# Piecewise-linear softmax weights: row maximum subtracted on TensorE, slopes carried in diagonal matrices, another engine order

## Chip, cores and metric

The program runs on one core of one Trainium2 chip. The metric is device time in microseconds (us) for one execution of the whole program, a small tower of four attention layers and four feed-forward layers over 2784 tokens of width 192. The change touches one stage of the second attention layer (the "pla" stage, `14_pla_...` in the names of the trace).

## The reference, cut to what matters

Scores of 12 heads are turned into attention weights by a softmax whose exponential is a table of straight lines (twelve pieces on -10 to 0, the last of them never chosen), after the shifted scores are put on a grid of 2^-26:

```python
scores = jnp.einsum('bhqd,bhkd->bhqk', q, k) * scale
def pla_softmax(scores):
    m = jnp.max(scores, axis=-1, keepdims=True)
    shifted = to_fixed_point(scores - m, 32, 26)      # round(x * 2**26), clipped, / 2**26
    xc = jnp.clip(shifted, -10.0, 0.0)
    idx = jnp.clip(jnp.searchsorted(PLA_A, xc, side='right') - 1, 0, PLA_A.shape[0] - 2)
    exps = PLA_M[idx] * xc + PLA_C[idx]
    sm = exps / (jnp.sum(exps, axis=-1, keepdims=True) + 1e-09)
    return quant(to_fixed_point(sm, 16, 15))
```

The pieces are 10/12 wide, so three of them span 2.5, and lines that lie 2.5 apart differ by the factor exp(-2.5). The kernel uses that: it moves each shifted score up by a whole number of steps of 2.5 into the pieces 8 to 10, evaluates those three lines, and multiplies by exp(-2.5 x steps).

## The kernel before, in words

`pla_stage` (L2483), called from `l1_attn` (L2925), works in 16 units of two batches each. One unit is a tile of 128 partitions by 1479 columns: 17 chunks of 87 keys, one row maximum for each chunk and partition. In PSUM such a tile lies in four banks, three with 435 columns (`wide`) and one with 174 (`rest`), so most PSUM reads are two instructions. Five engines run their own program, ordered by semaphores; each engine takes its instructions strictly in the order written out in the loops at the end of its function.

For a unit j:

- SyncE spreads the queries of a unit into block form with 12 DMAs (`heads.spread`), two units ahead of the scores at most.
- TensorE: `score(j)` puts the scores in the PSUM tile `ps` (bf16, short). It may overwrite `ps` once VectorE has taken the unit before (`taken`).
- VectorE, `take_off_top` (L2605): the row maximum (two reductions, L2608, L2610), the maximum times the scale (L2612), scores times scale minus maximum into `raw` (two scalar_tensor_tensor from PSUM, L2617, L2621), and the clamp at -10 that also writes integers into the same memory, `less` (L2624).
- ScalarE: `count`, the number of steps (L2581), and `fall`, exp(-2.5 x count) (L2585).
- VectorE, `shift` (L2637): `v` = `less` + 2.5 x `count`, two buffers.
- ScalarE: three lines over `v`, each a full pass with its own slope and offset: `mid` (L2589), `high` (L2591), `low` (L2593), two buffers each.
- VectorE, `cut` (L2628, L2630): `mid` and `high` are set to zero below their edges.
- TensorE, `add_up` (L2539): low, mid and high are added in the PSUM tile `line`, by matmuls with the identity, in fp32. One such pass over a tile is four matmuls in the source and eight in the trace, since fp32 takes two each (six of L2543, two of L2544).
- VectorE, `scale_line` (L2647): `line` times `fall` into `f`; `sum_up` (L2655 to L2662): the row sums and their reciprocals.
- ScalarE, `share_out` (L2573): `f` times the reciprocal into the 16-bit weights, 17 instructions, two units later.

The order on VectorE in an iteration is: take_off_top(j), cut(j-1), shift(j), sum_up(j-2), scale_line(j-1). On TensorE: low, mid, high of unit j-1, then score(j+1). On ScalarE: count, fall, mid, high, low of unit j, then share_out(j-2).

## Time and profile before

| | us |
|---|---|
| median of three runs | 2383.24 (2379.29 to 2392.43) |
| the profiled execution | 2381.72 |
| its span in the trace | 2379.3 |

The first row is the number that a changed kernel is held against. The profiled execution is a single one of the same program, and its span is what the trace covers of it, 2.4 us less than its device time. The pla stage lies between about 816 and 1055 us of that span.

### The profile page before, as it was taken

Reading aid. Unit: us, or ns where it says so; the run is one execution under the profiler, and the core shown is the slowest. Engines: PE = TensorE matmul, PEld = TensorE weight load, DVE = VectorE, ACT = ScalarE, POOL = GpSimd, SP = SyncE. Lnnn points to the kernel's source line nnn. Section 1 sums busy time; section 2 is a strip of 40 time slices with the busy share of each in tenths; the row PEclk is TensorE's granted clock in tenths of the full one; section 3 lists DMA queues with packets and bytes.
Section 4 is the critical chain, followed back from the end, with each engine's and each line's share of the span. In section 5 each row is a group of like instructions: output and inputs, shape, how many; then the busy total and the mean of one; then the engine's idle time right before and its main releaser. Section 6 shows DMA issues by size and latency. Waiting matters only on the chain. (4 is left out here: it accounts for less than half of the span.)

```text
span 2379.3 us, 35751 instructions
## 1 busy us (share of the span) xinstructions
PE 1676.9 (70%) x12022; PEld 1359.0 (57%) x12038; DVE 1323.9 (56%) x2732; ACT 1044.3 (44%) x2115; POOL 344.1 (14%) x417
## 2 busy tenths in 40 slices
PE   3588879947751377656589686664793699469995
PEld 2266658636641244336579563443683598369995
DVE  6599962350147989978712467997326211542223
ACT  4477742302224678876112147884322254312221
POOL 0000000006630000001043100000000342034431
PEclk9799969877875588987689896775897699679998
DMA  3200010304440000000467300000003453446775
GB/s 85 69 19 18 21 26 4 83 24 136 138 157 1 4 6 6 5 1 2 124 215 215 125 4 8 7 4 1 13 1 109 141 181 116 138 133 223 225 215 190
DMA packets 137245, 189.81 MB, mean 80 GB/s; under 512 B 51661, under 2 KB 111214, under 8 KB 137070
## 3 DMA queue, kind: packets, MB, share of 16 engines
q1 hardware_dynamic: 116289, 146.91, 20.2%
q0 software_dynamic: 15360, 36.72, 5.3%
q10 hardware_dynamic: 5420, 3.91, 0.6%
q8 instruction: 102, 1.67, 0.3%
q14 instruction: 74, 0.60, 0.1%
HBM read 150.21 MB, written 33.68 MB: 77 GB/s over the span
## 5 line engine op out<-in xcount | busy, mean ns | idle before, releaser
L989 DVE TENSOR_TENSOR 36_l3f_mlp_hidden<-36_l3f_mlp_gate,36_l3f_mlp_first 128x512 f32<-128x512 f32 x51 | 35.1, 688 | 185.3 <-ACT 36_l3f_mlp_gate L967 104.6
L882 PE MATMUL 36_l3f_mlp_first<-36_l3f_mlp_xT,36_l3f_mlp_w 128*128 128x128 f32 x816 | 101.5, 278 | 1.9 <-issue 1.9
L1005 DVE TENSOR_SCALAR 9_l0f_mlp_y<-9_l0f_mlp_second,l0f_routing_weight 128x192 f32<-128x192 f32 x51 | 20.4, 416 | 142.7 <-PE 9_l0f_mlp_second L896 63.1
L882 PEld LDWEIGHTS 36_l3f_mlp_first<-36_l3f_mlp_xT,36_l3f_mlp_w 128*128 128x128 f32 x816 | 97.0, 195 | 1.6 <-issue 1.6
L1245 PE MATMUL 2_performer_p_u<-perf_proj,2_performer_yT 128*87 128x512 f32 (+1 forms) x204 | 88.8, 577 | 10.6 <-DVE 2_performer_arg L1406 9.4
L967 ACT ACTIVATE 36_l3f_mlp_gate<-36_l3f_mlp_first 128x512 f32<-128x512 f32 x51 | 30.5, 598 | 137.5 <-PE 36_l3f_mlp_first L887 128.3
L1003 DVE TENSOR_TENSOR 32_l3a_mlp_y<-32_l3a_mlp_second,l3a_experts_b_rows 128x192 f32<-128x192 f32 x29 | 10.4, 358 | 136.8 <-issue 102.2
L896 PE MATMUL 36_l3f_mlp_second<-l3f_experts_w,36_l3f_mlp_hidden 128*128 x408 | 80.9, 342 | 0.0
L989 DVE TENSOR_TENSOR 22_l1f_mlp_hidden<-22_l1f_mlp_gate,22_l1f_mlp_first 128x512 f32<-128x512 f32 x29 | 20.0, 688 | 106.4 <-ACT 22_l1f_mlp_gate L967 85.5
L963 ACT ACTIVATE 32_l3a_mlp_hidden<-32_l3a_mlp_first,l3a_experts_b_cols 128x128 f32<-128x128 f32 x174 | 48.3, 378 | 65.9 <-PE 32_l3a_mlp_first L887 51.7
L2573 ACT ACTIVATE l1a_p<-14_pla_f,l1a_recip 128x87 int16<-128x87 f32 x272 | 71.7, 356 | 4.9 <-DVE l1a_recip L2662 4.9
L2543 PE MATMUL 14_pla_line<-14_pla_low,ident 128*128 128x435 f32 x96 | 50.5, 673 | 29.9 <-ACT 14_pla_low L2593 27.6
L896 PE MATMUL 9_l0f_mlp_second<-l0f_experts_w,9_l0f_mlp_hidden 128*128 x204 | 55.4, 401 | 22.2 <-issue 12.2
L856 POOL DMA_INDIRECT l3f_results<-36_l3f_mlp_y,l3f_routing_put x51 | 50.3, 987 | 136.0 <-DVE 36_l3f_mlp_y L1005 136.0
L896 PEld LDWEIGHTS 36_l3f_mlp_second<-l3f_experts_w,36_l3f_mlp_hidden 128*128 128x128 f32 x408 | 65.9, 192 | 6.5 <-issue 0.5
L896 PE MATMUL 32_l3a_mlp_second<-l3a_experts_w,32_l3a_mlp_hidden 128*128 x348 | 66.0, 341 | 2.4 <-ACT 32_l3a_mlp_hidden L963 2.4
L2543 PE MATMUL 14_pla_line<-14_pla_mid,ident 128*128 128x435 f32 x96 | 41.1, 564 | 36.2 <-DVE 14_pla_mid L2628 36.2
L963 ACT ACTIVATE 9_l0f_mlp_hidden<-9_l0f_mlp_first,l0f_experts_b_cols 128x128 f32<-128x128 f32 x102 | 32.1, 364 | 76.5 <-PE 9_l0f_mlp_first L887 43.0
L1245 PEld LDWEIGHTS 2_performer_p_u<-perf_proj,2_performer_yT 128*87 128x87 f32 x204 | 31.8, 169 | 56.4 <-issue 53.8
L930 ACT ACT_TABLE_LOAD x4 | 5.1, 1283 | 133.1 <-PEq L605 92.9
L887 PE MATMUL 36_l3f_mlp_first<-36_l3f_mlp_xT,36_l3f_mlp_w 64*128 64x128 f32 x816 | 60.5, 287 | 0.8 <-issue 0.8
L896 PEld LDWEIGHTS 32_l3a_mlp_second<-l3a_experts_w,32_l3a_mlp_hidden 128*128 128x128 f32 x348 | 57.4, 194 | 6.1 <-issue 2.9
(910 smaller groups left out, 4950.3 us busy)
## 6 DMA issues: line engine op xcount, KB each, us to landing
36_l3f_mlp_w<-in_L_ffn_w_dram SPq DMA_DIRECT2D x51, 768.0 KB
22_l1f_mlp_w<-in_L_ffn_w_dram SPq DMA_DIRECT2D x29, 768.0 KB
32_l3a_mlp_w<-in_L_attn_W_dram SPq DMA_DIRECT2D x29, 576.0 KB
9_l0f_mlp_w<-in_L_ffn_down_w_dram SPq DMA_DIRECT2D x51, 192.0 KB
l3a_experts_w<-in_L_attn_W_dram SPq DMA_DIRECT2D x8, 576.0 KB
l1a_blocks<-l1a_qkb SPq DMA_DIRECT2D x192, 5.4 KB, 1.8
l1f_experts_w<-in_L_ffn_w_dram SPq DMA_DIRECT2D x8, 384.0 KB, 6.3
l2a_blocks<-l2a_qkb SPq DMA_DIRECT2D x192, 5.4 KB, 1.8
```

Source lines behind the costliest of these rows:

```text
L856: nc.gpsimd.indirect_dma_start(route.results, to(i), y[i % NY][:], None).then_inc(put[i % NY], 16)
L882: nc.tensor.matmul(to(t + a * PAIRS), of[:, t + a * PAIRS, :], at[:, 0, :], start=(t == 0), stop=True, skip_group_check=True)
L887: ins = nc.tensor.matmul(to(t + a * PAIRS), of[rows, 2 * PAIRS + t, :], at[rows, 1, :], start=False, stop=True, skip_group_check=True)
L896: ins = nc.tensor.matmul(second[j % 2][:, 0:D], hidden[j % 2][:, t, :], ex.w2[:, ds(expert[j], 1), t, :].rearrange("p a w -> p (a w)"), st ...
L963: ins = nc.scalar.activation(out[:, t], src[:, t // PAIRS, t % PAIRS, :], func, bias=ex.b1_cols[:, ds(e, 1), t])
L967: nc.scalar.activation(out[:], src[:, 0, 0:HT, :], func).then_inc(done, 1)
L989: v.tensor_tensor(hidden[j % 2][:], gate[j % 2][:], first[j % 2][1][:, 0, 0:HT, :], ALU.mult).then_inc(hidden_done, 1)
L1003: ins = v.tensor_tensor(y[i % NY][:], of, ex.b2_rows[:, ds(e, 1), :].rearrange("p a w -> p (a w)"), ALU.add)
L1005: ins = v.tensor_scalar(y[i % NY][:], of, route.weight[:, i:i + 1], None, ALU.mult)
L1245: ins = t.matmul(p_u[:, k, 0:(EIGHT - h) * M], yT[b % 2][:, k, :], proj[:, h:EIGHT, :].rearrange("p h m -> p (h m)"), start=True, stop=True)
L2543: nc.tensor.matmul(to_w[:, n], kit.ident[:], of_w[:, n], start=start, stop=stop)
L2573: ins = a(P[:, j, n, :], f[j % 2][:, n * NT:(n + 1) * NT], ACT.Copy, scale=recip[:, j, n:n + 1])
```

## The change

The same weights are computed with other steps, and the work is handed to the engines in another order.

- The row maximum is taken of the raw scores (`find_top`), without the multiplication by the scale. TensorE subtracts it inside PSUM: `take_off_top` adds minus one times the maximum, repeated along the 87 keys, to `ps` with a diagonal matrix `minus` (four fp32 matmuls in the source). ScalarE then copies the difference out times the scale (`take`, two activations).
- The clamp (`clamp`) also adds a constant HOME, so that zero of the moved value lies where lines 8 and 9 cross.
- The slopes go into three diagonal matrices `by_low`, `by_mid`, `by_high`, made once at the start by four small tensor_scalar instructions (with `minus`). So low needs no instruction before TensorE, mid is one cut of `v`, and high is `v` plus a constant on ScalarE (`move_high`) and a cut. The common constant BASE is added in `scale_line`, which becomes a scalar_tensor_tensor.
- `v`, `mid` and `high` have one buffer instead of two.
- The loops are rewritten: scores and the subtraction run two units ahead of the lines, low one unit ahead, sum_up follows scale_line of the same unit, and share_out comes one unit later instead of two.

```diff
-    edge = [float(np.float32(a) * np.float32(UNIT)) for a in A]
+    across_89, across_910 = ((c[n + 1] - c[n]) / (m[n + 1] - m[n]) for n in (8, 9))
+    HOME = float(np.float32(across_89 * UNIT))
+    GAP = float((across_910 - across_89) * UNIT)
+    LEAST_V = 64.0 * math.ceil((HOME - 10.0 * UNIT) / 64.0)
+    BASE = float(c[8] - m[8] * across_89)
+    edge = [float(np.float32(float(np.float32(a) * np.float32(UNIT)) + HOME)) for a in A]
...
-        v_row = [kit.sb(ctx, f"v{u}", [128, UW]) for u in range(2)]
+        v_row, mid, high = (kit.sb(ctx, n, [128, UW]) for n in ("v", "mid", "high"))
-        low, mid, high = ([kit.sb(ctx, f"{n}{u}", [128, UW]) for u in range(2)] for n in ("low", "mid", "high"))
...
-        bias = kit.sb(ctx, "bias", [128, 4])
+        bias = kit.sb(ctx, "bias", [128, 2])
+        minus, by_low, by_mid, by_high = (kit.sb(ctx, n, [128, 128]) for n in ("minus", "by_low", "by_mid", "by_high"))
...
-            for k, value in enumerate((c[8], c[9] - c[8], c[10] - c[9], A[8] / STEP + 0.5)):
+            for k, value in enumerate((A[8] / STEP + 0.5 + HOME / (STEP * UNIT), GAP)):
...
-                    pe.wait_ge(taken, j)
+                    pe.wait_ge(raw_ready, j)
...
-            def add_up(part, start, stop):
+            def take_off_top(j):
+                pe.wait_ge(top_found, 2 * j + 2)
+                wide, rest = in_banks(ps)
+                for n in range(3):
+                    nc.tensor.matmul(wide[:, n], minus[:], across(top[:, n * PER_BANK:(n + 1) * PER_BANK], 2, NT), start=False,
+                                     stop=True, skip_group_check=True)
+                nc.tensor.matmul(rest, minus[:], across(top[:, 3 * PER_BANK:CHUNKS], 2, NT), start=False, stop=True,
+                                 skip_group_check=True).then_inc(less_done, 1)
+            def add_up(by, part, start, stop):
                 to_w, to_r = in_banks(line)
                 of_w, of_r = in_row(part)
                 for n in range(3):
-                    nc.tensor.matmul(to_w[:, n], kit.ident[:], of_w[:, n], start=start, stop=stop)
-                return nc.tensor.matmul(to_r, kit.ident[:], of_r, start=start, stop=stop)
-
-            pe.wait_ge(cleared, 1)
+                    nc.tensor.matmul(to_w[:, n], by[:], of_w[:, n], start=start, stop=stop)
+                return nc.tensor.matmul(to_r, by[:], of_r, start=start, stop=stop)
+
+            def low_line(j):
+                pe.wait_ge(v_ready, j + 1)
+                if j >= 1:
+                    pe.wait_ge(f_ready, j)
+                add_up(by_low, v_row, True, False).then_inc(low_done, 1)
+
+            def mid_line(j):
+                pe.wait_ge(mid_cut, j + 1)
+                add_up(by_mid, mid, False, False).then_inc(mid_done, 1)
+
+            def high_line(j):
+                pe.wait_ge(high_cut, j + 1)
+                add_up(by_high, high, False, True).then_inc(line_done, 1)
+
+            pe.wait_ge(cleared, 5)
             score(0)
-            for j in range(UNITS + 1):
-                i = j - 1
-                if i >= 0:
-                    pe.wait_ge(low_ready, i + 1)
-                    if i >= 1:
-                        pe.wait_ge(f_ready, i)
-                    add_up(low[i % 2], True, False)
-                    pe.wait_ge(mid_cut, i + 1)
-                    add_up(mid[i % 2], False, False)
-                    pe.wait_ge(high_cut, i + 1)
-                    add_up(high[i % 2], False, True).then_inc(line_done, 1)
-                if j + 1 < UNITS:
-                    score(j + 1)
+            for j in range(-2, U):
+                if has(j + 2) and j + 2 >= 1:
+                    score(j + 2)
+                if has(j):
+                    mid_line(j)
+                    high_line(j)
+                if has(j + 2):
+                    take_off_top(j + 2)
+                if has(j + 1):
+                    low_line(j + 1)
 
...
-            act.wait_ge(made, 4)
+            act.wait_ge(made, 2)
...
+            def take(j):
+                act.wait_ge(less_done, j + 1)
+                if j >= 1:
+                    act.wait_ge(v_ready, j)
+                for to, of in zip(in_row(raw), in_banks(ps)):
+                    ins = a(to, of, ACT.Copy, scale=scale)
+                ins.then_inc(raw_ready, 1)
+
+            def count_steps(j):
+                act.wait_ge(less_ready, j + 1)
+                a(count[:], less, ACT.Relu, bias=bias[:, 0:1], scale=-1.0 / (STEP * UNIT)).then_inc(count_ready, 1)
+                act.wait_ge(count_ready, j + 1)
+                if j >= 2:
+                    act.wait_ge(f_ready, j - 1)
+                a(fall[j % 2][:], count[:], ACT.Exp, scale=-STEP).then_inc(fall_ready, 1)
 
...
-            for j in range(UNITS):
-                u = j % 2
-                act.wait_ge(less_ready, j + 1)
+            def move_high(j):
+                act.wait_ge(v_ready, j + 1)
                 if j >= 1:
-                    act.wait_ge(fall_ready, j)
-                a(count[:], less, ACT.Relu, bias=bias[:, 3:4], scale=-1.0 / (STEP * UNIT)).then_inc(count_ready, 1)
-                act.wait_ge(count_ready, j + 1)
-                if j >= 2:
-                    act.wait_ge(f_ready, j - 1)
-                a(fall[u][:], count[:], ACT.Exp, scale=-STEP).then_inc(fall_ready, 1)
-                act.wait_ge(v_ready, j + 1)
-                if j >= 2:
-                    act.wait_ge(line_done, j - 1)
-                a(mid[u][:], v_row[u][:], ACT.Identity, bias=bias[:, 1:2],
-                  scale=float((m[9] - m[8]) / UNIT)).then_inc(mid_ready, 1)
-                a(high[u][:], v_row[u][:], ACT.Identity, bias=bias[:, 2:3],
-                  scale=float((m[10] - m[9]) / UNIT)).then_inc(high_ready, 1)
-                a(low[u][:], v_row[u][:], ACT.Identity, bias=bias[:, 0:1], scale=float(m[8] / UNIT)).then_inc(low_ready, 1)
-                if j >= 2:
-                    share_out(j - 2)
-            share_out(UNITS - 2)
-            share_out(UNITS - 1)
-            act.wait_ge(stored, UNITS)
+                    act.wait_ge(line_done, j)
+                a(high[:], v_row[:], ACT.Identity, bias=bias[:, 1:2]).then_inc(high_ready, 1)
+
+            for j in range(-2, U + 1):
+                if has(j + 1):
+                    count_steps(j + 1)
+                if has(j - 1):
+                    share_out(j - 1)
+                if has(j + 1):
+                    move_high(j + 1)
+                if has(j + 2):
+                    take(j + 2)
+            act.wait_ge(stored, U)
...
-            def take_off_top(j):
+            def find_top(j):
                 wide, rest = in_banks(ps)
                 dve.wait_ge(scores_done, j + 1)
+                if j >= 1:
+                    dve.wait_ge(less_done, j)
                 v.tensor_reduce(top[:, 0:15].rearrange("r (c n) -> r c n", c=3),
                                 wide.rearrange("r c (n k) -> r c n k", k=NT), AX.X, ALU.max).then_inc(top_found, 1)
                 v.tensor_reduce(top[:, 15:CHUNKS], by_chunk(rest), AX.X, ALU.max).then_inc(top_found, 1)
-                dve.wait_ge(top_found, 2 * j + 2)
-                v.tensor_scalar(top[:], top[:], scale, None, ALU.mult).then_inc(top_ready, 1)
-                dve.wait_ge(top_ready, j + 1)
+
+            def clamp(j):
+                dve.wait_ge(raw_ready, j + 1)
+                v.tensor_scalar(less, raw[:], HOME, LEAST_V, ALU.add, ALU.max).then_inc(less_ready, 1)
+
+            def cut(j):
+                dve.wait_ge(v_ready, j + 1)
                 if j >= 1:
-                    dve.wait_ge(v_ready, j)
-                to_w, to_r = in_row(raw)
-                v.scalar_tensor_tensor(to_w.rearrange("r c (n k) -> r c n k", k=NT),
-                                       wide.rearrange("r c (n k) -> r c n k", k=NT), scale,
-                                       across(top[:, 0:15].rearrange("r (c n) -> r c n", c=3), 3, NT),
-                                       ALU.mult, ALU.subtract)
-                v.scalar_tensor_tensor(by_chunk(to_r), by_chunk(rest), scale, across(top[:, 15:CHUNKS], 2, NT),
-                                       ALU.mult, ALU.subtract).then_inc(taken, 1)
-                dve.wait_ge(taken, j + 1)
-                v.tensor_scalar(less, raw[:], -10.0 * UNIT, None, ALU.max).then_inc(less_ready, 1)
-
-            def cut(j):
-                dve.wait_ge(mid_ready, j + 1)
-                v.scalar_tensor_tensor(mid[j % 2][:], v_row[j % 2][:], edge[9], mid[j % 2][:], ALU.is_ge, ALU.mult).then_inc(mid_cut, 1)
+                    dve.wait_ge(mid_done, j)
+                v.scalar_tensor_tensor(mid[:], v_row[:], edge[9], v_row[:], ALU.is_ge, ALU.mult).then_inc(mid_cut, 1)
                 dve.wait_ge(high_ready, j + 1)
-                v.scalar_tensor_tensor(high[j % 2][:], v_row[j % 2][:], edge[10], high[j % 2][:], ALU.is_ge, ALU.mult).then_inc(high_cut, 1)
+                v.scalar_tensor_tensor(high[:], v_row[:], edge[10], high[:], ALU.is_ge, ALU.mult).then_inc(high_cut, 1)
 
             def shift(j):
                 dve.wait_ge(count_ready, j + 1)
-                if j >= 2:
-                    dve.wait_ge(low_ready, j - 1)
-                    dve.wait_ge(high_cut, j - 1)
-                v.scalar_tensor_tensor(v_row[j % 2][:], count[:], STEP * UNIT, less, ALU.mult,
-                                       ALU.add).then_inc(v_ready, 1)
+                if j >= 1:
+                    dve.wait_ge(low_done, j)
+                    dve.wait_ge(high_cut, j)
+                v.scalar_tensor_tensor(v_row[:], count[:], STEP * UNIT, less, ALU.mult, ALU.add).then_inc(v_ready, 1)
 
...
-                    ins = v.tensor_tensor(to, of, by, ALU.mult)
+                    ins = v.scalar_tensor_tensor(to, of, BASE, by, ALU.add, ALU.mult)
...
             v.memset(ps[:], 0.0).then_inc(cleared, 1)
-            dve.wait_ge(cleared, 1)
-            for j in range(UNITS + 2):
-                if j < UNITS:
-                    take_off_top(j)
-                if 1 <= j <= UNITS:
-                    cut(j - 1)
-                if j < UNITS:
-                    shift(j)
-                if j >= 2:
-                    sum_up(j - 2)
-                if 1 <= j <= UNITS:
-                    scale_line(j - 1)
+            for to, by in ((minus, -1.0), (by_low, m[8] / UNIT), (by_mid, (m[9] - m[8]) / UNIT), (by_high, (m[10] - m[9]) / UNIT)):
+                v.tensor_scalar(to[:], kit.ident[:], float(by), None, ALU.mult).then_inc(cleared, 1)
+            dve.wait_ge(cleared, 5)
+            for j in range(-2, U):
+                if has(j + 1):
+                    clamp(j + 1)
+                if has(j):
+                    cut(j)
+                if has(j + 2):
+                    find_top(j + 2)
+                if has(j + 1):
+                    shift(j + 1)
+                if has(j):
+                    scale_line(j)
+                    sum_up(j)
```

## Rows read from the trace of the kernel before

**Rows 1.** The page's first part: engine, busy us, share of the span, instructions.

```profile
PE 1676.9 (70%) x12022; PEld 1359.0 (57%) x12038; DVE 1323.9 (56%) x2732; ACT 1044.3 (44%) x2115; POOL 344.1 (14%) x417
```

**Rows 2.** Busy time by stretch: stretch, its length, engines' busy us, granted clock, DMA.

```profile
core 0: us, PE busy (x) PEld busy (x) DVE busy (x) ACT busy (x) POOL busy (x), PEclk, DMA share, GB/s
942.00:956.00 14.00, 10.77 (x46) 5.90 (x45) 13.79 (x17) 12.11 (x25) 0.00 (x0) 0.88 0.03 5
...
984.00:998.00 14.00, 9.19 (x46) 5.30 (x45) 13.79 (x16) 12.10 (x25) 0.00 (x0) 1.00 0.03 5
```

**Rows 3.** Timeline, one unit on VectorE: start us, us, instruction.

```profile
931.08 0.93 DVE L2624 TENSOR_SCALAR 14_pla_raw<-14_pla_raw 128x1479 int32<-128x1479 f32 x1
931.92 1.69 DVE L2628 SCALAR_TENSOR_TENSOR 14_pla_mid<-14_pla_v,14_pla_mid 128x1479 f32<-128x1479 f32 x1
...
935.14 1.69 DVE L2637 SCALAR_TENSOR_TENSOR 14_pla_v<-14_pla_count,14_pla_raw 128x1479 f32<-128x1479 int32 x1
...
936.75 1.68 DVE L2655 TENSOR_REDUCE 14_pla_parts<-14_pla_f 128x51 f32<-128x1479 f32 x1
...
939.10 1.70 DVE L2647 TENSOR_TENSOR 14_pla_f<-14_pla_line,14_pla_fall 128x1305 f32<-128x1305 f32 x2
...
940.71 1.51 DVE L2608 TENSOR_REDUCE 14_pla_top<-14_pla_ps 128x15 f32<-128x1305 f32 x1
...
942.50 0.24 DVE L2612 TENSOR_SCALAR 14_pla_top<-14_pla_top,l1a_sc 128x17 f32<-128x17 f32 x1
...
942.78 1.58 DVE L2617 SCALAR_TENSOR_TENSOR 14_pla_raw<-14_pla_ps,l1a_sc,14_pla_top 128x1305 f32<-128x1305 f32 x1
...
944.69 0.93 DVE L2624 TENSOR_SCALAR 14_pla_raw<-14_pla_raw 128x1479 int32<-128x1479 f32 x1
```

**Rows 4.** Timeline, the same unit's line passes on TensorE, idle time before in brackets.

```profile
933.67 2.47 PE L2543 MATMUL 14_pla_line<-14_pla_mid,ident 128*128 128x435 f32 x6 [1.63 <-DVE 14_pla_mid L2628]
...
936.27 2.36 PE L2543 MATMUL 14_pla_line<-14_pla_high,ident 128*128 128x435 f32 x6
...
938.46 0.46 PE L2544 MATMUL 14_pla_line<-14_pla_high,ident 128*128 128x174 f32 x2
...
941.29 3.76 PE L2543 MATMUL 14_pla_line<-14_pla_low,ident 128*128 128x435 f32 x6 [1.58 <-ACT 14_pla_low L2593]
```

**Rows 5.** Timeline, ScalarE in the same unit.

```profile
939.72 1.51 ACT L2593 ACTIVATE 14_pla_low<-14_pla_v,14_pla_bias 128x1479 f32<-128x1479 f32 x1
...
941.14 4.49 ACT L2573 ACTIVATE l1a_p<-14_pla_f,l1a_recip 128x87 int16<-128x87 f32 x17
```

**Rows 6.** Timeline, ScalarE in a later attention stage, score banks taken from PSUM.

```profile
1500.57 1.34 ACT L3306 ACTIVATE 25_log_int_raw<-25_log_int_ps,l2a_con 128x1305 int32<-128x1305 f32 x1
1501.80 0.40 ACT L3307 ACTIVATE 25_log_int_raw<-25_log_int_ps,l2a_con 128x174 int32<-128x174 f32 x1
```

**Rows 7.** Groups by form, TensorE in that later stage: busy us, mean ns.

```profile
L3255 PE MATMUL 25_log_int_mid<-25_log_int_top,25_log_int_minus 128*128 128x440 bf16 x48 | 23.0, 534 | 0.0
...
L3253 PE MATMUL 25_log_int_mid<-25_log_int_score,identb 128*128 128x512 bf16 x18 | 10.0, 579 | 45.7 <-ACT 25_log_int_square L3334 44.4 <-DVE 25_log_int_top L3390 1.3
```

**Rows 8.** Waits of the DMA queue in the stage: us in total, times, longest.

```profile
SPq L2452 <- PE 14_pla_ps L2424: 69.2, 12, 7.4
```

**Rows 9.** Timeline, the stage's first two units.

```profile
819.99 1.52 DVE L2608 TENSOR_REDUCE 14_pla_top<-14_pla_ps 128x15 f32<-128x1305 f32 x1 [1.74 <-PE 14_pla_ps L2424]
...
832.10 0.93 DVE L2624 TENSOR_SCALAR 14_pla_raw<-14_pla_raw 128x1479 int32<-128x1479 f32 x1
...
832.65 4.34 PE L2543 MATMUL 14_pla_line<-14_pla_low,ident 128*128 128x435 f32 x6 [6.32 <-ACT 14_pla_low L2593]
```

**Rows 10.** Timeline, the stage's last units.

```profile
1022.99 2.46 PE L2543 MATMUL 14_pla_line<-14_pla_low,ident 128*128 128x435 f32 x6 [1.58 <-ACT 14_pla_low L2593]
...
1026.39 0.93 DVE L2624 TENSOR_SCALAR 14_pla_raw<-14_pla_raw 128x1479 int32<-128x1479 f32 x1
...
1050.34 4.49 ACT L2573 ACTIVATE l1a_p<-14_pla_f,l1a_recip 128x87 int16<-128x87 f32 x17 [4.13 <-DVE l1a_recip L2662]
```

More of the change, by code:

```diff
@@ L2491, in pla_stage @@
     STEP = 2.5
-    edge = [float(np.float32(a) * np.float32(UNIT)) for a in A]
+    across_89, across_910 = ((c[n + 1] - c[n]) / (m[n + 1] - m[n]) for n in (8, 9))
[4 more added lines that the diff above has]
+    edge = [float(np.float32(float(np.float32(a) * np.float32(UNIT)) + HOME)) for a in A]
+    U = UNITS
     with kit.stage("pla") as ctx:
@@ L2504, in pla_stage @@
         parts = kit.sb(ctx, "parts", [128, CHUNKS, 3])
-        bias = kit.sb(ctx, "bias", [128, 4])
+        bias = kit.sb(ctx, "bias", [128, 2])
+        minus, by_low, by_mid, by_high = (kit.sb(ctx, n, [128, 128]) for n in ("minus", "by_low", "by_mid", "by_high"))
         ps = kit.ps(ctx, "ps", [128, 4, 512])
         line = kit.ps(ctx, "line", [128, 4, 512])
-        names = ("made", "scores_done", "top_found", "top_ready", "taken", "less_ready", "count_ready", "fall_ready",
-                 "v_ready", "mid_ready", "high_ready", "low_ready", "mid_cut", "high_cut", "line_done", "f_ready",
+        names = ("made", "scores_done", "top_found", "less_done", "raw_ready", "less_ready", "count_ready", "fall_ready",
+                 "v_ready", "high_ready", "mid_cut", "high_cut", "low_done", "mid_done", "line_done", "f_ready",
                  "parts_ready", "summed", "total_ready", "recip_ready", "stored", "cleared")
-        (made, scores_done, top_found, top_ready, taken, less_ready, count_ready, fall_ready, v_ready, mid_ready,
-         high_ready, low_ready, mid_cut, high_cut, line_done, f_ready, parts_ready, summed, total_ready,
+        (made, scores_done, top_found, less_done, raw_ready, less_ready, count_ready, fall_ready, v_ready, high_ready,
+         mid_cut, high_cut, low_done, mid_done, line_done, f_ready, parts_ready, summed, total_ready,
          recip_ready, stored, cleared) = (kit.sem(ctx, n) for n in names)
@@ L2516, in pla_stage @@
         K_v = QK[:, 1].rearrange("p k (b t) -> p k b t", t=NT)
+        has = lambda j: 0 <= j < U
         @block.gpsimd
         def _(pool):
-            for k, value in enumerate((c[8], c[9] - c[8], c[10] - c[9], A[8] / STEP + 0.5)):
+            for k, value in enumerate((A[8] / STEP + 0.5 + HOME / (STEP * UNIT), GAP)):
                 nc.gpsimd.memset(bias[:, k:k + 1], float(value)).then_inc(made, 1)
@@ L2524, in _ @@
         def _(sp):
-            for j in range(1, UNITS):
+            for j in range(1, U):
                 if j >= 2:
```

## The prediction

> **What bounds the kernel now.** The page's first part [rows 1] says only that no engine is busy for more than 70% of the whole span, so the stage has to be read by itself. The busy time by stretch comes next [rows 2]: in the middle of the pla stage VectorE is busy for 13.79 of 14 us, TensorE for 9.2 to 10.8 and ScalarE for 12.1. VectorE bounds this stage. Its timeline over one unit [rows 3] shows where that goes: it starts the clamp at 931.08 and again at 944.69, a period of 13.61 us with no idle time worth naming. By the starts of successive instructions one unit costs VectorE: clamp 0.84, two cuts 3.22 (931.92 to 935.14), shift 1.61, sums and reciprocal 2.35 (936.75 to 939.10), scale_line 1.61, the two maxima 1.79 (940.71 to 942.50), maximum times scale 0.28, subtraction 1.91. TensorE meanwhile waits for VectorE's cut and for ScalarE's low, 1.63 and 1.58 us in this unit [rows 4]. From the clamp of unit 1 at 832.10 [rows 9] to that of unit 15 at 1026.39 [rows 10] it is 194.3 us, 13.88 a unit, and from there 28.44 us to the end of the last share_out (1054.83). The DMA queue waits some 5.8 us for the scores in each unit [rows 8], so the 12 transfers leave slack and stay two units ahead in the new order.
>
> **What the change takes from VectorE.** It removes the scaled maximum (0.28) and the subtraction (1.91). Clamp, cuts, shift, maxima and sums keep their forms and prices; the clamp gets a second constant, in the same instruction. scale_line turns from tensor_tensor into scalar_tensor_tensor out of PSUM: it can cost 1.61 as now or the 1.91 of the subtraction, which is that very instruction from the same kind of banks with the same two shapes [rows 3]. I take 1.91. VectorE's own work is then 0.84 + 3.22 + 1.79 + 1.61 + 1.91 + 2.35 = 11.72 us a unit, 1.9 less than now.
>
> **What it gives to the others.** ScalarE loses two of three line passes (1.51 each [rows 5]) and gains `take`: 1.23 from start to start for the wide part plus 0.40, so 1.63, as a later stage pays for the same copy from PSUM [rows 6]. Its work of 12.1 in 14 us, or 11.8 a unit, falls to about 10.4. TensorE gains a fourth fp32 pass. A pass is 2.5 to 2.6 us at the full clock: mid starts at 933.67, high at 936.27, and both are over at 938.92, 5.25 us for two [rows 4]. The moving operand of the new pass is the maximum repeated along the keys, which no fp32 matmul shows; in a later stage such a repeated operand costs 534 ns for 440 columns against 579 ns for 512 plain ones [rows 7], 1.21 against 1.13 ns a column. The shorter matmul's fixed part accounts for that, and if it did not, 7% of a pass is under 0.2 us. Four passes and the scores (about a microsecond) make 11 us a unit.
>
> No engine is over 11.8, so what counts is the chain from one clamp to the next. I lay one unit out with the clamp at 0, as the new code orders it:
>
> 1. VectorE: clamp to 0.84, first cut to 2.53 (1.69).
> 2. TensorE: scores of unit j+2 are long done, so mid_line starts 0.06 after the cut, as at 931.92 + 1.69 to 933.67 [rows 3, 4]; mid and high end at 2.59 + 5.25 = 7.84. The second cut ends at 4.14, in time for high.
> 3. VectorE has meanwhile done second cut, maxima and shift, and stands free at 0.84 + 3.22 + 1.79 + 1.61 = 7.46. scale_line waits for the line until 7.90: a new stall of 0.44. Queued behind it are sum_up and the next clamp. scale_line ends at 9.81, sum_up at 12.16.
> 4. TensorE goes on with the subtraction of unit j+2 (its maxima were ready by 5.9) from 7.84 to 10.34. ScalarE has spent 0.9 to about 9.7 on count, fall, share_out and move_high, so `take` starts at 10.40 and ends at 12.03; the next clamp could start at 12.07.
> 5. low_line of unit j+1 runs behind it (f is ready at 9.8) until 12.85, then the scores until 13.9, which is 1.7 in the next unit. mid_line there starts at 2.6, so neither delays it; TensorE's only gap is about 0.9.
>
> Both chains end within 0.1 us: 12.07 over TensorE and ScalarE, 12.16 over scale_line and the sums. The period is the larger, 12.16. A scale_line at 1.61 would leave 12.07; slower hand-overs or a slower repeated operand could make it 12.5. Waits that the one-buffer tiles add cost nothing here, each because its releaser is early: shift waits for low_done (0.85 into the unit) and runs at 5.86, move_high waits for line_done (7.84) with ScalarE busy until about 8.3, the first cut waits for a mid_done of the unit before. If low were late by over 5 us, shift would pay.
>
> **Start and end.** The four diagonal matrices are tensor_scalar on 128 columns; the clamp takes 0.93 for 1479 [rows 3], so with a fixed part like the 0.24 of L2612 each is about 0.2, 0.7 together, before the first score. Then the first maxima end at 819.99 + 0.7 + 1.8 = 822.5 [rows 9]. The first subtraction runs on a clock that is still at 1.2 GHz, as the first low pass does, 4.34 us for six matmuls against 2.36 [rows 9, 4]; with its last two some 4.9, to 827.4. take to 829.1, score(1) 1.7, second maxima to 832.6, second subtraction to 835.2 at 2.4 GHz or 837.5 at 1.2. take(1) is also queued behind move_high(0), which waits for the shift behind the maxima: ready at 835.8. So the clamp of unit 1 comes between 837.5 and 839.2. TensorE has idled for most of this start, so I take 839: 7 us later than the 832.10 of now. At the end: clamp of unit 15 at 0, sum_up(14) done at 12.2, cut to 13.9, mid and high to 19.2, scale_line and sums to 23.6, share_out(15) 4.49 [rows 10] to 28.1, which is 0.3 less than the 28.44 of now.
>
> **Sum.** 14 x (13.88 - 12.16) = 24.1 saved, 7 lost at the start, 0.3 saved at the end: 17.4 us. The stages behind start with a wait for this one and no transfer is in flight, so they move as a block. 2381.72 - 17.4 = 2364.3 for the profiled execution; the median of the runs lies 1.5 above that, so 2366.
>
> **The clock.** Now, the granted clock is 0.88 in one stretch of the stage and 1.00 in another, with the same work [rows 2]: in the first the low pass falls to 1.2 GHz (3.76 us for six matmuls after 1.58 us idle [rows 4]), in the second it does not (2.46 after the same 1.58 [rows 10]). So two gaps of 1.6 us a unit stand on the edge. The new order leaves one gap of 0.9, which speaks for the full clock throughout. The Trainium skill ("TensorE: Matmul & The Clock Gate", "A second HAM failure mode: psum-queue depth-cycling") says that short idle times between groups of matmuls can be enough to make the clock go back and forth. That is the first rival below; this trace agrees for the gaps of now in one stretch and not in the other.
>
> **Rivals.**
>
> - *The clock falls in every unit* (ends slower). Three of the four passes now lie on the chain. One of them at 1.2 GHz adds some 2.3 us (4.34 + 0.3 against 2.36) to a period: 14 x 2.3 = 32, less 17.4, makes 15 us slower, 2398. It decides from seven or eight such passes on, where the gain is gone. Against it: the smaller gap. 0.12.
> - *The loop is longer than laid out.* The unit now crosses engines five times, against a VectorE that never had to wait. If hand-overs, the repeated fp32 operand or a queued instruction make the period 13.0, the saving is 14 x 0.88 = 12.3, less 6.7: 2377. From 12.55 on it is within 0.5%. Against it: hand-overs of 0.06 in the rows. 0.20.
> - *VectorE's own work is the whole period*, because the line is ready earlier than I lay out and scale_line costs 1.61: 11.4 to 11.7, 31 to 34 saved, less 6.7: 24 to 28, or about 2358. Against it: the chain over TensorE and ScalarE stands at 12.07. 0.08.
>
> **How the numbers follow.** The forecast has 0.60, with a period of 12.0 to 12.5: 2362 to 2371. A measurement of this kernel tells 0.5%, 12 us, from no change. Faster by more: 0.57 of the forecast and 0.08 of the third rival, 0.65. Within: 0.03, the second rival's 0.20 and 0.02 of the first, 0.25. Slower: 0.10. The range takes in the second and third rival and a few microseconds by which medians differ, and leaves the clock out: 2356 to 2386.
>
> **What would show it.** The clamp's starts 12.1 to 12.2 us apart from unit 2 on; scale_line some 0.2 us longer in sum, after an idle time of about 0.4 released by TensorE; `take` at 1.34 and 0.40; granted clock 1.00 from the second unit on; TensorE's gaps before mid_line under 1 us; the clamp of unit 1 seven microseconds later. I am wrong if a pass of the chain shows 3.7 us or more for six matmuls in most units, or if VectorE waits for `raw` rather than for the line.

## The result and the profile after

| | before | after |
|---|---|---|
| median of the runs of one call | 2387.84 us (4 runs, 2379.29 to 2393.2) | 2359.93 us (4 runs, 2358.91 to 2368.74) |
| profiled execution: own time, span | 2381.72, 2379.3 us | 2360.82, 2358.7 us |
| pla stage, first clear to last share_out | 238.35 us | 219.37 us |
| clamp to clamp, mean of units 1 to 15 | 13.88 us | 12.04 us |

The ratio of the times is 0.9898 [0.9872, 0.9924]. The stage is counted from the start of the clear of the score banks (the memset of ps: 816.48 before, 819.69 after) to the end of share_out(15). It is 19.0 us shorter, and the profiled executions differ by 20.9. Three of before's four runs are those of the front section, with a median of 2383.24; against that number after's median is 23.3 us lower.

The page's first part, after (engine, busy us, share of the span, instructions):

```profile
PE 1698.8 (72%) x12150; PEld 1375.5 (58%) x12166; DVE 1290.5 (55%) x2688; ACT 1022.7 (43%) x2115; POOL 343.4 (15%) x415
```

Against [rows 1] VectorE is busy for 33 us less and TensorE for 22 more. Whether that is time saved can't be read here. The busy time by stretch, for the two stretches of [rows 2]:

```profile
core 0: us, PE busy (x) PEld busy (x) DVE busy (x) ACT busy (x) POOL busy (x), PEclk, DMA share, GB/s
...
942.00:956.00 14.00, 12.97 (x60) 7.61 (x59) 13.41 (x14) 12.36 (x28) 0.00 (x0) 1.00 0.05 7
984.00:998.00 14.00, 12.97 (x60) 7.71 (x59) 13.38 (x15) 11.76 (x24) 0.00 (x0) 1.00 0.01 1
```

Three engines now stand between 11.8 and 13.4 of 14, and the granted clock is 1.00 in both, where one of the two had 0.88. VectorE has lost its full row of work: it idles about 0.6 us in 14. One unit of the timeline, VectorE, TensorE and ScalarE together (start us, us, instruction, idle time before it in brackets):

```profile
926.76 0.93 DVE L2654 TENSOR_SCALAR 14_pla_raw<-14_pla_raw 128x1479 int32<-128x1479 f32 x1
...
927.60 1.69 DVE L2660 SCALAR_TENSOR_TENSOR 14_pla_mid<-14_pla_v 128x1479 f32<-128x1479 f32 x1
...
929.35 2.46 PE L2561 MATMUL 14_pla_line<-14_pla_mid,14_pla_by_mid 128*128 128x435 f32 x6 [1.03 <-DVE 14_pla_mid L2660]
...
931.94 2.36 PE L2561 MATMUL 14_pla_line<-14_pla_high,14_pla_by_high 128*128 128x435 f32 x6
...
934.43 2.35 PE L2552 MATMUL 14_pla_ps<-14_pla_top,14_pla_minus 128*128 128x435 f32 x6
934.63 1.76 DVE L2678 SCALAR_TENSOR_TENSOR 14_pla_f<-14_pla_line,14_pla_fall 128x1305 f32<-128x1305 f32 x2 [0.46 <-PE 14_pla_line L2562]
...
936.43 1.69 DVE L2686 TENSOR_REDUCE 14_pla_parts<-14_pla_f 128x51 f32<-128x1479 f32 x1
...
936.92 2.35 PE L2561 MATMUL 14_pla_line<-14_pla_v,14_pla_by_low 128*128 128x435 f32 x6
937.12 1.64 ACT L2604 ACTIVATE 14_pla_raw<-14_pla_ps,l1a_sc 128x1305 f32<-128x1305 f32 x2 [0.60 <-PE 14_pla_ps L2554]
...
938.61 0.26 DVE L2693 RECIPROCAL l1a_recip<-14_pla_total 128x17 f32<-128x17 f32 x1
938.80 0.93 DVE L2654 TENSOR_SCALAR 14_pla_raw<-14_pla_raw 128x1479 int32<-128x1479 f32 x1
```

This is the unit that the prediction laid out, with the clamp at 926.76 as its zero. The first cut frees TensorE, which runs mid, high and the subtraction without a pause. scale_line waits 0.46 for the line, where [rows 3] show no wait. `take` ends at 938.76. The reciprocal starts at 938.61, and in e1 below the next instruction starts 0.18 after it (938.38 to 938.56), which would be 938.79 here. So both chains end in the next clamp within 0.1 us; the clamp has no wait in brackets, and the trace doesn't tell which of the two came last. The period is 12.04 where [rows 3] had 13.61. In the waits from 850 to 1010 us (waiting for what: us in total, times, longest) the new stall is there in each of the 14 units, 0.45 on average:

```profile
DVE 14_pla_f L2678 <- PE 14_pla_line L2562: 6.3, 14, 0.5
```

The timeline at the start and at the end of the stage:

```profile
819.69 1.76 DVE L2695 MEMSET 14_pla_ps<- 128x2048 f32 x1 [1.13 <-PEq L2903]
...
825.49 4.72 PE L2552 MATMUL 14_pla_ps<-14_pla_top,14_pla_minus 128*128 128x435 f32 x6 [1.95 <-DVE 14_pla_top L2650]
...
835.43 4.72 PE L2552 MATMUL 14_pla_ps<-14_pla_top,14_pla_minus 128*128 128x435 f32 x6 [1.87 <-DVE 14_pla_top L2650]
...
842.44 0.93 DVE L2654 TENSOR_SCALAR 14_pla_raw<-14_pla_raw 128x1479 int32<-128x1479 f32 x1 [5.46 <-ACT 14_pla_raw L2604]
...
1011.06 0.93 DVE L2654 TENSOR_SCALAR 14_pla_raw<-14_pla_raw 128x1479 int32<-128x1479 f32 x1
...
1034.57 4.49 ACT L2618 ACTIVATE l1a_p<-14_pla_f,l1a_recip 128x87 int16<-128x87 f32 x17 [6.84 <-DVE l1a_recip L2693]
```

The clamp of unit 1 starts 22.75 us after the clear, against 15.62 before (832.10 [rows 9] less 816.48): 7.1 later. Both first subtractions run at 1.2 GHz (4.72 us against 2.35 in the loop); the run with work at the start, below, shows what that costs. From the clamp of unit 15 to the end are 28.0 us, 0.4 less than before [rows 10]. 14 x (13.88 - 12.044) - 7.13 + 0.44 = 19.0, the whole difference of the stage.

Not all of the 25.7 us that the loop saves come from the steady period. Before, the first two of the 14 units take 15.87 and 15.00 us, since scale_line waits there for the first lines; the other twelve take 13.61 to 13.63. The timeline of before:

```profile
842.32 1.76 DVE L2647 TENSOR_TENSOR 14_pla_f<-14_pla_line,14_pla_fall 128x1305 f32<-128x1305 f32 x2 [4.46 <-PE 14_pla_line L2544]
...
857.32 1.76 DVE L2647 TENSOR_TENSOR 14_pla_f<-14_pla_line,14_pla_fall 128x1305 f32<-128x1305 f32 x2 [1.23 <-PE 14_pla_line L2544]
```

After, all 14 take 12.04 or 12.05. So 14 x (13.62 - 12.044) = 22.0 us come from the period, and 3.7 from two long units that are gone.

### The profile page after: what moved, and what is told of

Its sections match the earlier page's. It is cut to its first block and busy times, and to the rows that moved or that the text cites. A ratio compares the mean times of both kernels' runs of the same rounds, so it can differ in the third digit from the quotient of the medians.

```text
span 2358.7 us, 35978 instructions
## 1 busy us (share of the span) xinstructions
PE 1698.8 (72%) x12150; PEld 1375.5 (58%) x12166; DVE 1290.5 (55%) x2688; ACT 1022.7 (43%) x2115; POOL 343.4 (15%) x415
## 5 line engine op out<-in xcount | busy, mean ns | idle before, releaser
L1245 PE MATMUL 2_performer_p_u<-perf_proj,2_performer_yT 128*87 128x512 f32 (+1 forms) x204 | 94.1, 605 | 10.6 <-DVE 2_performer_arg L1406 9.5
L882 PE MATMUL 22_l1f_mlp_first<-22_l1f_mlp_xT,22_l1f_mlp_w 128*128 128x128 f32 x464 | 58.6, 280 | 1.0 <-issue 0.9
```

Of the source, the lines that this page charges most:

```text
L882: nc.tensor.matmul(to(t + a * PAIRS), of[:, t + a * PAIRS, :], at[:, 0, :], start=(t == 0), stop=True, skip_group_check=True)
L1245: ins = t.matmul(p_u[:, k, 0:(EIGHT - h) * M], yT[b % 2][:, k, :], proj[:, h:EIGHT, :].rearrange("p h m -> p (h m)"), start=True, stop=True)
```

## The experiments

Theory A, the prediction's: the chain clamp, first cut, mid and high passes, scale_line, sums sets the period, a second chain over the subtraction and `take` ends with it, and VectorE's own work is shorter than both. B to E are its rivals in this stage; F came up on the way and is about the stage behind. "Stage" and "period" in the table are of each profiled execution, counted as above; the ratio is to runs of the kernel before on the same chip.

| run | period | stage | median us (runs) | ratio |
|---|---|---|---|---|
| e6_before_again | 13.88 | 238.4 | 2386.25 (10) | 1.0008 [0.9991, 1.0026] |
| e0_after | 12.05 | 218.3 | 2360.42 (4) | 0.9889 [0.9871, 0.9908] |
| e1_cut_first | 11.70 | 212.1 | 2354.30 (4) | 0.9875 [0.9829, 0.9921] |
| e2_vector_subtracts | 13.54 | 233.5 | 2380.79 (9) | 1.0007 [0.9976, 1.0037] |
| e3_scalar_slopes | 14.06 | 250.0 | 2394.20 (10) | 1.0032 [1.0017, 1.0048] |
| e4_warm_start | 12.04 | 214.3 | 2356.56 (5) | 0.9882 [0.9854, 0.9910] |
| e5_together | 11.69 | 203.0 | 2349.14 (6) | 0.9878 [0.9843, 0.9913] |
| e7_warm_context | 11.69 | 202.9 | 2350.63 (5) | 0.9861 [0.9842, 0.9880] |
| e8_together_again | 11.69 | 202.6 | 2351.15 (6) | 0.9859 [0.9830, 0.9888] |

**The changed kernel and the one before, again.** No edit in either.

> The changed kernel itself, for the same chip as the others. Every theory: about 2360 us, clamps of the stage 12.04 us apart, the stage 19 us shorter than before.

> The kernel before once more, for a second profile of it: the stage again 238.4 us from its first memset to the end of the last share_out, and the stretches ahead of it and behind it show by how much they differ between two executions of the same program (theory A: by several us, which is what is left of the measured gain beside the stage's own 19). Rival E: they are the same as in the first profile, and the change shortens stages that it does not touch.

Period and stage repeat to 0.1 and 1.1 us. The 1.1 lie at the start of after: the clamp of unit 1 comes 21.63 us after the clear in e0 and not 22.75, and the first subtraction is shorter than the 4.72 us that it took in after:

```profile
831.09 4.11 PE L2552 MATMUL 14_pla_ps<-14_pla_top,14_pla_minus 128*128 128x435 f32 x6 [1.95 <-DVE 14_pla_top L2650]
```

What repeats less is the code that nothing touched: the clear starts at 816.5 and 825.6 us in the two executions of before, at 819.7 and 825.3 in those of after. So the stage is the finer gauge, and the experiments are read by it first.

**The first cut ahead of the clamp.** VectorE's order alone: TensorE gets its first cut before the clamp and not after it.

```diff
...
+                if has(j):
+                    cut_mid(j)
                 if has(j + 1):
                     clamp(j + 1)
                 if has(j):
-                    cut(j)
+                    cut_high(j)
```

> Only VectorE's order changes: the first cut stands ahead of the clamp. Theory A (a chain that starts at the clamp and runs over the first cut, two line passes, scale_line and the sums sets the period): the line passes start 0.85 us earlier, the wait of 0.45 us at scale_line goes, the period falls from 12.04 to VectorE's own 11.6 us, 14 x 0.44 = 6 us less: 2354. Rival B (VectorE's own instructions set it already, the short waits are no part of it): 12.04 and 2360 as before.

The timeline of e1 in one unit:

```profile
927.13 1.64 DVE L2660 SCALAR_TENSOR_TENSOR 14_pla_mid<-14_pla_v 128x1479 f32<-128x1479 f32 x1
...
928.68 0.92 DVE L2654 TENSOR_SCALAR 14_pla_raw<-14_pla_raw 128x1479 int32<-128x1479 f32 x1
...
934.40 1.76 DVE L2680 SCALAR_TENSOR_TENSOR 14_pla_f<-14_pla_line,14_pla_fall 128x1305 f32<-128x1305 f32 x2
...
938.56 1.64 DVE L2660 SCALAR_TENSOR_TENSOR 14_pla_mid<-14_pla_v 128x1479 f32<-128x1479 f32 x1
...
940.11 0.92 DVE L2654 TENSOR_SCALAR 14_pla_raw<-14_pla_raw 128x1479 int32<-128x1479 f32 x1
```

The stall at scale_line is gone here, and the unit takes 11.43 us from clamp to clamp, the work of VectorE itself. There are no fewer instructions and none is shorter by more than 0.05 us, so the order was what set 12.04: theory A. It doesn't tell which of A's two chains was last, since both start with the first cut and gain alike. The mean is 11.70 and not the 11.6 expected, because in seven units, the first and then every second one, VectorE still waits 0.35 to 1.1 us for the line. TensorE shows why in the unit behind the one above: the first cut ends at 940.20, but the scores stand ahead of mid in TensorE's order, and they wait for `take`, so mid starts at 940.98:

```profile
940.10 0.79 PE L2418 MATMUL 14_pla_ps<-l1a_qkb,l1a_blocks 96*128 96x87 bf16 x16 [0.76 <-ACT 14_pla_raw L2604]
```

The stage is 6 to 7 us shorter than after's; the medians agree with that, though their intervals overlap.

**The subtraction back on VectorE.** The pass on TensorE and `take` go; the slopes stay in the diagonal matrices.

```diff
...
                 if has(j + 1):
                     shift(j + 1)
+                if has(j + 2):
+                    take_off_top(j + 2)
                 if has(j):
                     scale_line(j)
```

> The subtraction of the maximum goes back to VectorE (0.28 + 1.91 us a unit), the new order and the diagonal slopes stay. Theory A: VectorE's own work of 11.6 + 2.2 = 13.8 us is then longer than the chain and sets the period: 14 x 1.75 = 24.5 us more in the loop, some 5 less at the start, which has no passes of TensorE in it: 2379. Rival C (the gain came from the order, two units of look-ahead, and not from the subtraction): a period near 12 and 2355 to 2360.

The timeline of e2, VectorE:

```profile
928.33 0.87 DVE L2650 TENSOR_SCALAR 14_pla_raw<-14_pla_raw 128x1479 int32<-128x1479 f32 x1
...
935.87 1.58 DVE L2641 SCALAR_TENSOR_TENSOR 14_pla_raw<-14_pla_ps,l1a_sc,14_pla_top 128x1305 f32<-128x1305 f32 x1
...
937.36 0.39 DVE L2645 SCALAR_TENSOR_TENSOR 14_pla_raw<-14_pla_ps,l1a_sc,14_pla_top 128x174 f32<-128x174 f32 x1
937.67 1.75 DVE L2674 SCALAR_TENSOR_TENSOR 14_pla_f<-14_pla_line,14_pla_fall 128x1305 f32<-128x1305 f32 x2
...
941.82 0.87 DVE L2650 TENSOR_SCALAR 14_pla_raw<-14_pla_raw 128x1479 int32<-128x1479 f32 x1
```

VectorE is full again, 13.49 us from clamp to clamp with no wait at scale_line; rival C's 12 is false. 13.8 was expected: the scaled maximum and the subtraction cost 2.06 here (935.61 to 937.67) and not 2.19, and the rest of VectorE's work is 11.4 and not 11.6. Half of the change (slopes and order) brings 4.9 us in the stage and nothing that the runs can tell.

**The slopes back on ScalarE.** Three passes over v as before; the subtraction stays on TensorE. The weights aren't after's (each product is now rounded before TensorE adds it, which may be why), so the run counts for its time alone.

```diff
-                a(high[:], v_row[:], ACT.Identity, bias=bias[:, 1:2]).then_inc(high_ready, 1)
+                a(mid[:], v_row[:], ACT.Copy, scale=float((m[9] - m[8]) / UNIT)).then_inc(mid_ready, 1)
+                a(high[:], v_row[:], ACT.Identity, bias=bias[:, 1:2], scale=float((m[10] - m[9]) / UNIT)).then_inc(high_ready, 1)
+                a(low[:], v_row[:], ACT.Copy, scale=float(m[8] / UNIT)).then_inc(low_ready, 1)
...
```

> The slopes go back to ScalarE, which makes low, mid and high in three passes again; subtraction on TensorE and new order stay. Theory A: ScalarE's chain clamp, count, fall, share_out, three passes, take, clamp is 0.89 + 1.56 + 1.41 + 4.49 + 4.35 + 1.64 = 14.4 us and sets the period: 14 x 2.35 = 33 us more, 2392. Rival C, or any theory in which the diagonal slopes are idle decoration: 2360.

The timeline of e3, the clamp and the ScalarE passes ahead of it:

```profile
928.57 0.93 DVE L2656 TENSOR_SCALAR 14_pla_raw<-14_pla_raw 128x1479 int32<-128x1479 f32 x1 [1.56 <-ACT 14_pla_raw L2604]
...
936.83 1.42 ACT L2625 ACTIVATE 14_pla_mid<-14_pla_v 128x1479 f32<-128x1479 f32 x1
938.15 1.51 ACT L2626 ACTIVATE 14_pla_high<-14_pla_v,14_pla_bias 128x1479 f32<-128x1479 f32 x1
...
939.57 1.42 ACT L2627 ACTIVATE 14_pla_low<-14_pla_v 128x1479 f32<-128x1479 f32 x1
...
940.89 1.61 ACT L2604 ACTIVATE 14_pla_raw<-14_pla_ps,l1a_sc 128x1305 f32<-128x1305 f32 x2
942.54 0.93 DVE L2656 TENSOR_SCALAR 14_pla_raw<-14_pla_raw 128x1479 int32<-128x1479 f32 x1 [1.85 <-ACT 14_pla_raw L2604]
```

Now the clamp waits 1.6 to 1.9 us for `take`, which stands behind three passes on ScalarE: the engine is the bound, with 13.97 us in most units where 14.4 was expected, and the kernel is 8 us, 0.3%, slower than before. Each half alone leaves one engine full, VectorE in e2 and ScalarE in e3; only both together shorten the unit. The new order is in both of these runs; it wasn't tried without either half.

**Work for TensorE at the start.** 19 fp32 matmuls of 128 columns around the first two scores, into a line bank that is overwritten afterwards.

```diff
...
+            keep_busy(6)
             pe.wait_ge(cleared, 5)
             score(0)
+            keep_busy(4)
...
```

> The changed kernel with 19 small matmuls that nobody reads put into TensorE's idle stretches of the stage's first 15 us. Theory A: the first two subtractions ran at 1.2 GHz because TensorE had been idle, 5.3 us each where a pass takes 2.6; at 2.4 GHz the first saves 2.7 us and the second some 2.2, until take(1) waits for move_high(0) instead; the clamp of unit 1 comes 17.9 us after the stage's first memset, not 22.75: 2355. Rival D (the start is set by VectorE and ScalarE, or so few matmuls do not raise the clock): 22.7 and 2360.

The timeline of e4, the first two subtractions and the clamp of unit 1:

```profile
824.69 2.46 PE L2552 MATMUL 14_pla_ps<-14_pla_top,14_pla_minus 128*128 128x435 f32 x6 [0.62 <-DVE 14_pla_top L2660]
...
832.09 2.46 PE L2552 MATMUL 14_pla_ps<-14_pla_top,14_pla_minus 128*128 128x435 f32 x6 [0.78 <-DVE 14_pla_top L2660]
...
836.77 0.93 DVE L2664 TENSOR_SCALAR 14_pla_raw<-14_pla_raw 128x1479 int32<-128x1479 f32 x1 [3.12 <-ACT 14_pla_raw L2614]
```

Both passes run at 2.4 GHz, and the clamp comes 17.87 us after the clear (818.90): 4.9 us earlier than in after's profile, 3.8 earlier than in e0's. So of the six to seven microseconds that the start lost, four to five were the clock. The stage is 4 to 5 us shorter, but this one execution took 2376 us: it lost 20 us in the context stage behind, on which more below.

**Together, and the end shared.** e1 and e4, `take(1)` ahead of move_high(0), the last first-cut ahead of the last scale_line but one, and share_out(15) split between ScalarE (6 of 17 chunks) and VectorE (11).

```diff
...
-                for n in range(CHUNKS):
+                for n in range(CHUNKS if j < U - 1 else BY_ACT):
...
+            v.tensor_tensor(P[:, U - 1, n:CHUNKS, :], by_chunk(f[(U - 1) % 2][:])[:, n:CHUNKS, :],
+                            across(recip[:, U - 1, n:CHUNKS], 2, NT), ALU.mult).then_inc(shared, 1)
...
```

> First cut ahead of the clamp, the busy start, take(1) ahead of move_high(0), the last unit's first cut ahead of the wait of unit 14's scale_line, and the last share_out split between ScalarE (6 chunks) and VectorE (11). Theory A: the savings lie at different places and add: 6 in the loop, 5 to 6 at the start, 2 and 2.9 at the end, 16 in all: 2344. If they share a bound (rival B or D): 2350 to 2360.

The timeline at the end of e5's stage:

```profile
1022.61 1.66 ACT L2629 ACTIVATE l1a_p<-14_pla_f,l1a_recip 128x87 int16<-128x87 f32 x6 [5.16 <-DVE l1a_recip L2708]
1022.61 1.16 DVE L2732 TENSOR_TENSOR l1a_p<-14_pla_f,l1a_recip 128x957 int16<-128x957 f32 x1
```

The last step takes 1.66 us where it took 4.49, and the stage 203.0, 16.4 less than after's, where 16 were expected: the savings add. By place they are 4.9 in the loop, 5.1 at the start and 6.4 at the end (of these, e1 alone has 2.3), where 6, 5 to 6 and 4.9 were expected; that the sum fits better than its terms is luck. But two of the six runs took 2366 us, 15 to 23 more than the others, so the median, 2349.1, is nearer to the rivals' 2350 than to 2344, and only the stage decides.

**Dense matmuls ahead of the context stage.** e7 is e5 with 12 fp32 matmuls of 128 columns at the beginning of the next stage's TensorE program; e8 is e5 unchanged, on the same chip.

```diff
...
         def _(pe):
+            for _ in range(12):
+                nc.tensor.matmul(p_out[1][:, 0, 0:128], kit.ident[:, 0:NT], kit.ident[:], start=True, stop=True)
```

> The kernel of all edits together, with 12 dense fp32 matmuls that nobody reads at the start of the next stage (context). Theory F: the runs that take some 20 us longer are those in which that stage stays at 1.2 GHz to its end, as the profile of the warm start shows (95.6 us from its first turn to the next front stage, not 75.5); a dense stretch ahead of its small matmuls raises the clock, the context stage shows 1.00 from its first unit on, no run is 20 us longer, and the rest stay at 2344 to 2350. Rival G: the clock of that stage is a matter of chance or comes from elsewhere; a run in three is 20 us longer still.

> The same kernel as e5_together, on the same chip as the one with the dense stretch, to count the longer runs without it. Theory F: about one run in three near 2366, the others 2344 to 2351. Rival G: no more of them here than with the dense stretch.

Busy time by stretch in the context stage, first e7 and then e8:

```profile
1038.00:1045.00 7.00, 5.57 (x111) 5.27 (x110) 4.38 (x9) 6.74 (x10) 0.00 (x0) 1.00 0.00 0
1045.00:1052.00 7.00, 6.62 (x134) 6.38 (x132) 6.42 (x13) 6.47 (x11) 0.00 (x0) 1.00 0.01 2
```

```profile
1038.00:1045.00 7.00, 7.00 (x83) 7.00 (x82) 3.95 (x9) 4.20 (x6) 0.00 (x0) 0.50 0.01 2
...
1066.00:1073.00 7.00, 7.00 (x82) 7.00 (x81) 4.14 (x8) 4.00 (x7) 0.00 (x0) 0.50 0.00 0
```

In e8 TensorE is at 1.2 GHz in all five stretches of 7 us from 1038 to 1073 us, with no idle time in the trace, and gets 82 or 83 matmuls done in each where e7 has up to 134. The context stage takes 95.7 us against 75.2. e4 shows the same, 95.6; the other profiles have 75 to 78. That explains e4's and e8's profiled runs (theory F). e5 and e8 are the same program, and e5's profile shows 1.00 in the stretches from 1038 to 1066 us: nothing in the program decides between the two levels, which is what rival G says of the cause.

That the 12 matmuls prevent the slow case isn't settled: no run of e7 stands out (2346.8 to 2354.5), while of the 17 runs of e4, e5 and e8 five do, if their times are read so; if the edit did nothing, five runs without one would still come up about one time in six ((12/17)^5 = 0.18). One run of after (2368.74) and one of e1 (2369.28) stand out as well, and have no profile. Nor are the 12 matmuls free: they take 4.79 us, and the first turn comes 9.4 us after the end of share_out(15), against 6.0 in e5. From that end to the next front stage are 84.5 us in e7, 81.3 in e5 and 101.8 in e8, so the edit costs 3 us where the clock rises by itself and saves 17 where it doesn't. e7's median lies 31.5 us under before's on its chip, and e8's 31.0.

## Why the prediction held, point by point

- **The period** was to be 12.16 and is 12.04, a little under the 12.1 to 12.2 that was to be seen. The chain over `take` was to end 0.1 before the other and does so within 0.1. e1 shows that the order sets the period; the third rival (VectorE's own work is the period) is false for after, and true for e1's best units. The median of the runs, 2359.93, lies between that rival's 2358 and the forecast's own 2362 to 2371; only the period in the trace and the wait in it tell the two apart.
- **The stall** has the releaser that was named. That its size fits, 0.44 laid out and 0.45 measured, is luck in part: the forecast counts from where VectorE could start the next instruction, the trace from the end of shift (934.18). Counted like the forecast it is 0.53 (from 932.49 + 1.61 = 934.10 to 934.63), since VectorE is ready 0.12 sooner than laid out: the two maxima, taken at the 1.79 of the old order, cost 1.67 (930.82 to 932.49). They lie ahead of the wait, so this doesn't change the period.
- **The mis-sized term** is scale_line: taken at the 1.91 of the old subtraction, it costs 1.80 from its start to the sums (934.63 to 936.43), and 1.79 in e2 where it doesn't wait. With 1.80 the forecast's own chains would end at 12.05 and 12.07, so this term accounts for 0.09 of the 0.12 a unit, 1.3 of the 1.6 us by which the stage saved more than the 17.4 forecast; the rest is a chain over `take` that is 0.03 shorter than laid out. The other value that the forecast weighed, 1.61 as before, couldn't come with the new order whatever the form of the instruction: before, the 1.70 us of scale_line were followed by the maxima, which don't need its output and start 0.09 before its end (940.71 [rows 3]); now the sums follow, which need it, and start 0.04 after its 1.76 us. Why it takes 1.76 and not 1.70 wasn't tried.
- **The two long units** of before are in the forecast's 13.88, but nowhere in its account: rows 3, which it lays out, have 13.61. That the new order has no such units, which is worth 3.7 us, was assumed and not argued. It came out so.
- **The repeated fp32 operand**, which no row of before showed, costs nothing more: 2.35 us for six matmuls against 2.35 and 2.36 of plain passes. `take` costs 1.64; 1.63 was forecast [rows 6].
- **The start**: 7.1 us later against the 7 taken, and 6.0 in e0. The subtractions at 1.2 GHz were its largest part, as e4 shows. The end: 0.44 less, 0.3 forecast.
- **The clock**: 1.00 in both stretches of the loop, so the first rival (2398) is false. TensorE still has one gap in each unit, 1.03 us where about 0.9 was laid out and under 1 was to be seen. The reason that the forecast gave, the smaller gap, isn't shown. It read two gaps of 1.6 us a unit at either clock, but in the stretch of before that ran at 1.00 the gap ahead of mid is twice as long, as its timeline shows, and the one ahead of low still 1.58 [rows 10]:

```profile
1015.37 2.47 PE L2543 MATMUL 14_pla_line<-14_pla_mid,ident 128*128 128x435 f32 x6 [3.25 <-DVE 14_pla_mid L2628]
```

So the longer idle time went with the full clock there, and why the clock held in the new loop stays open. The Trainium skill ("TensorE: Matmul & The Clock Gate", "A second HAM failure mode: psum-queue depth-cycling") has short idle times between groups of matmuls make the clock swing; these two stretches, with a 1.03 us gap in each unit, don't show it.
- **The longer loop** (2377) is false: hand-overs cost what the rows of before had, and one buffer less for v, mid and high costs no wait in the unit shown.
- **What stays open**: the forecast for the profiled execution was 2364.3, and it took 2360.8. The stage explains 1.6 us of these 3.5; the rest lies in unchanged code ahead of and behind it, where two executions of one kernel differ by as much (span less stage: 2141.0 and 2144.7 for before, 2139.3 and 2142.8 for after). The medians differ by 23 to 28 us (24 by the ratio's 0.9898), the stage by 19 to 20: of the remainder nothing was shown to belong to the change.

## What to carry to other kernels

When work is taken from the engine that is full, lay one unit out with the new order: the gain ends at the chain that takes over (12.04 here, with 11.5 of VectorE's own work), and the order of two instructions on it can be worth more than a mis-sized term of the sum (0.34 us a unit in e1, against 0.11). Price an instruction by what follows it, too: on VectorE the maxima and scale_line cost 0.12 to 0.13 us more here when the next instruction needs their output than when it doesn't. Try each half of a change alone: here one half gave nothing that the runs can tell and the other a loss, because each left one engine full. A loop at its limit leaves its start and end as the next place to look: clock, first unit and last share gave 9 to 10 us here.

## What the runs showed of the hardware

TensorE's clock can stay at 1.2 GHz while the trace shows the engine busy without a break: 7.00 of 7.00 us in every stretch from 1038 to 1073 us in e8, for the same work that ran at 2.4 GHz in e7, in after and in e5, which is the same program as e8. About half of that busy time are transposes (17 of the 41 instructions of a unit), and the ends of matmuls are modelled in these profiles. In after the clock is 0.50 from 1042 to 1049 us and 1.00 from 1052 on. The slow case costs 20 us in a stage of 75. The Trainium skill ("TensorE: Matmul & The Clock Gate", "What's actually happening") says that the throttled state is the default and activity releases it. After's trace agrees with that; e8's stretches are busy by the trace and were not released, and no run here shows what made the difference.
